# State space and wide attention of a four-layer chain: softplus first, one decay product read out of another, and reciprocal roots by Ln and Exp

## The reference

```
dt = softplus(raw_dt + dt_bias);  a = -exp(A_log) * dt
xBC = silu(depthwise_conv(xBC, 4 taps) + bias)
y[t] = sum over s <= t of exp(sum of a from s+1 to t) * (C[t] . B[s]) * dt[s] * x[s]   + D * x
out = rmsnorm(y * silu(z)) @ W_out
```

```
qh, kh = rms_norm(q @ Wq), rms_norm(kv @ Wk)        # x * rsqrt(mean(x^2) + 1e-5) * w
attn   = softmax(mask(qh @ kh^T / 8));  out = (attn @ vh) @ Wo
```

## Time and profile before

| | |
|---|---|
| median of 3 runs | 2303.56 us (2299.27 to 2307.39) |
| profiled execution, its own time | 2310.8 us |
| its span in the profile | 2309.0 us |
| granted TensorE clock, mean | 0.904 of full speed |
| busy over the span | PE 83%, DVE 69%, ACT 57%, POOL 28% |
| chain that ended last | PE 50%, DVE 31%, issue 8%, POOL 5%, ACT 5% |
| state space | about 520 to 960 us |
| wide attention | about 1383 to 1800 us |

### The profile page before, as it was taken

How to read it: one execution, slowest core, us unless ns; L and a number is a source line. 1 busy time by engine, 2 the same in 40 slices (tenths; PEclk the granted TensorE clock), 3 DMA queues, 4 the chain that set the end, 5 groups by cost and what they waited for, 6 DMA issues and landing times.

```text
span 2309.0 us, 37826 instructions
## 1 busy us (share of the span) xinstructions
PE 1907.6 (83%) x13360; PEld 1271.5 (55%) x13360; DVE 1584.6 (69%) x3689; ACT 1307.4 (57%) x2688; POOL 646.3 (28%) x616
## 2 busy tenths in 40 slices
PE   7999766979999999849864388899888997679886
PEld 5777652446777777524452254556555676434465
DVE  5777685866767767458659948888888457568543
ACT  5777433766777777517755236676665312337622
POOL 3332003104433333342004532334334001131043
PEclk9999887999999999969986689999999898779897
DMA  4000005400000000034101000000000100254112
GB/s 191 1 2 2 1 0 152 141 34 5 1 1 1 1 1 1 1 91 147 56 8 68 0 1 1 1 1 1 1 1 1 52 4 1 95 159 132 43 35 78
DMA packets 80155, 87.39 MB, mean 38 GB/s; under 512 B 6578, under 2 KB 70115, under 8 KB 79073
## 3 DMA queue, kind: packets, MB, share of 16 engines
q1 hardware_dynamic: 78625, 82.49, 11.3%
q0 software_dynamic: 1344, 2.49, 0.4%
HBM read 54.39 MB, written 30.70 MB: 37 GB/s over the span
## 4 chain that ended last, share of the span: by engine, by line
PE 50%; DVE 31%; issue 8%; POOL 5%; ACT 5%; DMA 2%; SPq 0%; DVEq 0%; POOLq 0%; ACTq 0%
PE bank L469 42%; DVE scratch L1221 5%; PE bank L653 2%; DVE scratch L3045 2%; DVE scratch L3065 2%; PE bank L368 2%; POOL w_early L3241 1%; DVE stats L245 1%; PE bank L693 1%; POOL w_early L3236 1%; DVE w_keep L1893 1%; DVE w_early L2497 1%; PE bank L1190 1%; DVE XN L3089 1%; DMA scratch<-parts 1%
## 5 line engine op out<-in xcount | busy, mean ns | idle before, releaser
L469 PE MATMUL bank<-scratch 64*128 64x256 bf16 (+7 forms) x3056 | 340.9, 307 | 83.2 <-DMA scratch<-parts 39.8
L1221 DVE TENSOR_REDUCE scratch<-bank 128x2 f32<-128x512 f32 x384 | 244.6, 686 | 83.5 <-PE bank L469 80.6
L469 PEld LDWEIGHTS bank<-scratch 64*128 64x128 bf16 (+4 forms) x3056 | 183.9, 122 | 212.1 <-DVE scratch L1221 73.6
L469 PE MATMUL bank<-w_keep,scratch 128*128 128x128 f32 (+4 forms) x1760 | 246.6, 331 | 26.8 <-DVE scratch L1936 12.1
L469 PE MATMUL bank<-XNT,w_keep 128*128 128x256 f32 (+4 forms) x800 | 238.6, 438 | 6.8 <-POOL w_keep L2131 4.6
L1307 ACT ACTIVATE w_keep<-bank 128x512 f32<-128x512 f32 x384 | 212.5, 597 | 53.6 <-PE bank L469 45.7
L469 PEld LDWEIGHTS bank<-w_keep,scratch 128*128 128x128 f32 (+3 forms) x1760 | 183.7, 185 | 92.9 <-issue 63.5
L469 PE MATMUL bank<-w_early,scratch 64*128 64x256 f32 (+3 forms) x1152 | 168.9, 355 | 42.4 <-ACT w_early L3150 26.0
L469 PEld LDWEIGHTS bank<-XNT,w_keep 128*128 128x128 f32 x800 | 150.2, 197 | 59.9 <-issue 30.4
L469 PEld LDWEIGHTS bank<-w_early,scratch 64*128 64x128 f32 (+3 forms) x1152 | 122.6, 189 | 89.2 <-issue 32.3
L469 PE MATMUL bank<-w_keep 128*32 128x256 f32 (+1 forms) x1600 | 125.2, 388 | 8.8 <-ACT w_keep L1307 5.4
(11 more groups left out here) (452 smaller groups left out, 3974.5 us busy)
## 6 DMA issues: line engine op xcount, KB each, us to landing
scratch<-parts SPq DMA_DIRECT2D x24, 1024.0 KB, 5.0
parts<-scratch SPq DMA_DIRECT2D x192, 96.0 KB, 2.5
parts<-scratch SPq DMA_DIRECT2D x96, 64.0 KB, 2.1
w_early<-pack_l3f SPq DMA_DIRECT2D x1, 5206.0 KB, 16.3
w_keep<-pack_l2f SPq DMA_DIRECT2D x1, 2124.0 KB, 12.5
w_early<-pack_mamba SPq DMA_DIRECT2D x1, 2120.0 KB, 19.2
w_keep<-pack_l2x SPq DMA_DIRECT2D x1, 2049.0 KB, 7.8
w_keep<-taps SPq DMA_DIRECT2D x4, 512.0 KB, 5.6
```

Of the source, the lines that this page charges most:

```text
L469: return pe.matmul(out, lhsT, rhs, start=start, stop=stop, skip_group_check=True)
L1221: dve.tensor_reduce(neg[:, :, h], self.k.bank[5 - g % 2][:, :].rearrange("p (t s) -> p t s", s=S), AXX, ALU.max, negate=True).then_inc(*s. ...
```

## The change

In the state space:

- The product `after` (128x4) on PE is gone. The decays up to the half's end are the last column of each head's block in bank 5, which `decay_pe` writes anyway; ACT takes their exponential there, in a new small instruction (128x4) ahead of the first `decay_act`. `late_act` reads 256 columns in place of 260. POOL's `middle_pool` waits for `decay` in place of `late`.
- Tap 0 is the unshifted one (the former tap 3), and DVE reads it straight from bank 0. The other three follow from the padded buffer. PE's next `raw_pe` waits for that DVE instruction in place of ACT's copy.
- On DVE the softplus's start and its first four series steps stand ahead of `overlap_dve`.

In the wide attention:

- Both roots are Ln and Exp(-0.5 x) on ACT; DVE's reciprocals and the keys' scaling go, and one table set (preloaded once) serves the stage.
- KS and KD are split in two pieces: KS0 in step 1, KS1 and KR in step 2, KD0 in step 3, KD1 in step 4.
- V1, V3, T01 and T11 are copied by ACT.
- POOL squares the next batch's keys ahead of its scaling in steps 0 and 1.

```
@@ state space: late_pe, tap_dve
-        mm(pe, bank[:, S:S + H_SSM], self.k.w["after"], a3[:, 0, :]).then_inc(*s.scored.up("late", u))
+        m.then_inc(*s.scored.up("late", u))
...
-            pe.wait_ge(*s.stacked.at("raw", u - 1))
+            pe.wait_ge(*s.vector.at("tap", u - 1, 0, 1))
...
-                o = dve.tensor_scalar(yv[:, j, :], xv[:, j, 0:S], scale, None, ALU.mult)
+                o = dve.tensor_scalar(yv[:, j, :], self.two(self.k.bank[0][:, :])[:, j, :], scale, None, ALU.mult)
@@ state space: dve
+            if soft:
+                soft.start_dve(dve, n)
+                soft.series_dve(dve, n, 0, 4)
             if there(prep):
                 self.overlap_dve(dve, prep)
-            if soft:
-                soft.start_dve(dve, n)
-            if there(prep):
                 self.weights_dve(dve, prep)
-            if soft:
-                soft.series_dve(dve, n, 0, 4)
@@ state space: late_act, decay_act, middle_pool
-            act.wait_ge(*s.pool.at("xu", u - 2))
-        act.activation(self.late[u % 2], self.k.bank[2][:, 0:S + H_SSM], ACT.Exp).then_inc(*s.weighed.up("late", u))
+        act.activation(self.late[u % 2][:, 0:S], self.k.bank[2][:, 0:S], ACT.Exp).then_inc(*s.weighed.up("late", u))
...
+        if t == 0:
+            if u >= 2:
+                act.wait_ge(*s.pool.at("xu", u - 2))
+            ends = columns_of(self.k.bank[5][:, :], P - 1, (P, H_SSM))
+            act.activation(self.late[u % 2][:, S:S + H_SSM], ends, ACT.Exp)
...
-        pool.wait_ge(*s.weighed.at("late", u))
+        pool.wait_ge(*s.weighed.at("decay", u, 0))
@@ wide attention: schedule
-    SCHEDULE = (("P00", "P01", "Q0"), ("P10", "P11", "Q1"), ("Q2", "Q3", "KS"), ("M", "V0", "KR", "KD"), ("B0", "V1"),
-                ("T00", "T01", "X"), ("T10", "T11", "V2", "QR", "QD"), ("B1", "V3"))
+    SCHEDULE = (("P00", "P01", "Q0"), ("P10", "P11", "Q1", "KS0"), ("Q2", "Q3", "KS1", "KR"), ("M", "V0", "KD0"), ("B0", "V1", "KD1"),
+                ("T00", "T01", "X"), ("T10", "T11", "V2", "QR"), ("B1", "V3"))
+    ON_ACT = ("V1", "V3", "T01", "T11")
@@ wide attention: score_pe, values_pe, maximum_dve
-            pe.wait_ge(*self.read(("Q3", b)))
+            pe.wait_ge(*self.read(("T10", b)))
...
+            pe.wait_ge(*self.read(("V2", b)))
...
-            dve.wait_ge(*s.rstd.at("queries", b))
+            dve.wait_ge(*s.deviation.at("queries", b))
@@ wide attention: piece_act (KR; QR the same without bias)
-            act.activation(self.kms, self.kms, ACT.Sqrt).then_inc(*s.deviation.up("keys", b))
+            act.wait_ge(*s.stats.at("keys", b, 1))
+            act.activation(self.kms, self.kms, ACT.Ln, bias=k.small[:, 0:1], scale=1.0 / HW).then_inc(*s.scalar.up("keys", b))
+            act.wait_ge(*s.scalar.at("keys", b))
+            act.activation(self.kms, self.kms, ACT.Exp, scale=-0.5).then_inc(*s.deviation.up("keys", b))
@@ wide attention: pool
-            self.scale_pool(pool, p)
             if w in (0, 1) and b + 1 < B:
                 self.squares_pool(pool, b + 1, w)
+            self.scale_pool(pool, p)
@@ wide_attention: act
-        pre_norm_act(k, e, ACT.Exp)
+        pre_norm_act(k, e)
+        e.preload_act_table_set("natural_log_exp_and_others")
```

More of the change, by code:

```diff
@@ L2861, in __init__ @@
                         self.place[name, b] = d * NWIDE + step if d >= 0 else -1
-        on_pe = [piece for piece in self.place if piece[0] not in ("KS", "KR", "KD", "QR", "QD")]
+        on_pe = [piece for piece in self.place if piece[0] not in self.UNBANKED]
         self.number = {piece: n for n, piece in enumerate(on_pe)}
@@ L3075, in piece_dve @@
         digits = [int(x) for x in name[1:] if x.isdigit()]
[L3076 to L3083, removed]
-            dve.wait_ge(*s.deviation.at("keys", b))
[L3085 to L3088, removed]
-                dve.tensor_tensor(x, x, self.kms[:, t * H:(t + 1) * H].unsqueeze(2).to_broadcast([P, H, HW]), ALU.mult).then_inc(*s.normed.up("keys", b, t))
-        elif name == "QD":
-            dve.wait_ge(*s.deviation.at("queries", b))
-            dve.reciprocal(self.qms[b % 2], self.qms[b % 2]).then_inc(*s.rstd.up("queries", b))
+        if name[0:2] == "KS":
+            t = digits[0]
+            dve.wait_ge(*s.pool.at("squares", b, t))
+            dve.tensor_reduce(self.kms[:, t * H:(t + 1) * H], self.ksquares[t].rearrange("p (h d) -> p h d", d=HW), AXX,
+                              ALU.add).then_inc(*s.stats.up("keys", b, t))
+        elif name[0:2] == "KD":
+            t = digits[0]
+            x = self.raw[t].rearrange("p (h d) -> p h d", d=HW)
+            dve.wait_ge(*s.deviation.at("keys", b))
+            dve.tensor_tensor(x, x, self.kms[:, t * H:(t + 1) * H].unsqueeze(2).to_broadcast([P, H, HW]), ALU.mult).then_inc(*s.normed.up("keys", b, t))
+        elif name in self.ON_ACT:
+            pass
         elif name[0] == "X":
@@ L3172, in piece_act @@
         if name == "KR":
-            act.wait_ge(*s.variance.at("keys", b))
-            act.activation(self.kms, self.kms, ACT.Sqrt).then_inc(*s.deviation.up("keys", b))
+            act.wait_ge(*s.stats.at("keys", b, 1))
+            act.activation(self.kms, self.kms, ACT.Ln, bias=k.small[:, 0:1], scale=1.0 / HW).then_inc(*s.scalar.up("keys", b))
+            act.wait_ge(*s.scalar.at("keys", b))
+            act.activation(self.kms, self.kms, ACT.Exp, scale=-0.5).then_inc(*s.deviation.up("keys", b))
         elif name == "QR":
             act.wait_ge(*s.formed.at("X", b))
-            act.activation(self.qms[b % 2], self.qms[b % 2], ACT.Sqrt).then_inc(*s.deviation.up("queries", b))
+            act.activation(self.qms[b % 2], self.qms[b % 2], ACT.Ln).then_inc(*s.scalar.up("queries", b))
+            act.wait_ge(*s.scalar.at("queries", b))
+            act.activation(self.qms[b % 2], self.qms[b % 2], ACT.Exp, scale=-0.5).then_inc(*s.deviation.up("queries", b))
+        elif name[0] == "V" and name in self.ON_ACT:
+            t, part = divmod(digits[0], 2)
+            act.wait_ge(*s.projected.at(*piece))
+            if b >= 2:
+                act.wait_ge(*s.summed.at("v", (b - 1) * NWIDE - 1))
+            act.activation(self.values(b)[:, t, 8 * part:8 * part + 8, :], bank[:, :].rearrange("p (h d) -> p h d", d=HW), ACT.Copy,
+                           scale=self.keep[:, b * HALVES + t:b * HALVES + t + 1]).then_inc(*s.stacked.up(*piece))
+        elif name[0] == "T" and name in self.ON_ACT:
+            t, part = digits
+            act.wait_ge(*s.projected.at(*piece))
+            if b >= 2:
+                act.wait_ge(*s.scored.at("s", (b - 1) * NWIDE - 1, 1))
+            act.activation(self.side(self.K, b)[:, 4 * part:4 * part + 4, t * P:(t + 1) * P], bank[:, :].rearrange("p (w s) -> p w s", s=P),
+                           ACT.Copy).then_inc(*s.stacked.up(*piece))
         elif name[0] == "P":
```

19 lines of the change are left out of this document (10 added, 9 removed).

## The result

The changed kernel takes 2241.3 us, median of 4 runs (2238.2 to 2246.0), against 2303.8 for the kernel before; the ratio is 0.973, with a 95% interval of 0.970 to 0.976. That is 62.5 us less, where 57 was forecast; the forecast of 2247 lies 6 us above the measurement and the range holds it. The profiled execution took 2244.2 us, its span 2242.4 (before 2309.0), at a mean granted clock of 0.911 (before 0.904).

The account below looks back on a forecast made before the run. The prediction took DVE's in-order list, partly held by POOL, to bound even state-space iterations and wide-attention batches. Gains of 22.5 and 34.5 us, 57 in all, took 2303.6 to 2247; range 2220 to 2277.

Parts of the forecast that it names:

- What left the list: State space, even iterations: the softplus's start (2.27 us) and four series steps (0.72) leave DVE's list after the overlap.
- The late overlap: State space, even iterations: the softplus, moved ahead, makes DVE's overlap start 0.15 us late.
- the tap out of the bank: State space, even iterations: reading tap 0 from the bank instead of SBUF costs 0.26 us a pair.
- the hold of the series: State space, even iterations: the last three series steps meet POOL's instructions and take 0.93 us more; bounds 0 and 1.5.
- the reopened gap: State space, even iterations: a gap ahead of the weights, which L1594 had covered, reopens and costs 0.12 us.
- ACT's limit of 2.0: State space, even iterations: with DVE out of the way, ACT's own chain limits the gain to about 2.0 us.
- The holds: Wide attention: DVE instructions standing for POOL's (L3049, KD0, KD1) give back 2.25 us a batch; bounds 0 and 4.
- The reserve that is not gained: Wide attention: DVE reached step 0's maximum late without shortening PE's list, so 1.0 us a batch is not gained.
- No holds: Both stages: moved DVE instructions do not meet POOL's or slip by; gain 81 us, to 2223; chance 0.2.
- A new wait: Both stages: half the gain goes into new waits for series steps and divided pieces; gain 27, 2276; chance 0.2.
- Nothing: Ln and Exp might each load their table set, and PE absorb DVE's gain: within 0.3%; chance 0.05.
- Slower: Wide attention: POOL's squares, ahead of its scaling, wait for ACT's copy of P01 and delay PE: 2319; chance 0.05.

Follow-up runs that it names:

- 3: The changed kernel with the softplus's start and first four series steps back behind the overlap on DVE: 2256.3 us.
- 4: The changed kernel with the product `after` back on PE, one exponential of 260 columns and the old waits: 2228.7 us.
- 9: The changed kernel with Sqrt on ACT and reciprocals on DVE for both roots, so four table loads a batch: 2246.1 us.
- 8: The changed kernel with V1, V3, T01 and T11 copied by DVE again: 2239.7 us.
- 7: The changed kernel with POOL scaling first and squaring the next batch's keys after it, as before: 2276.0 us.
- 12: The kernel before with only POOL's order changed, squaring the next batch's keys ahead of its scaling: 2295.2 us against 2301.9 beside it.
- 5: The changed kernel with the first, unshifted tap read from the padded SBUF buffer in place of the bank: 2235.3 us.
- 10: The changed kernel with KD0 and KD1 each right behind the step's maximum on DVE, ahead of the inverse: 2231.6 us.
- 11: The changed kernel with the whole softplus and decays ahead of the overlap, and KD0, KD1 right behind the maximum: 2215.0 us against 2290.1, ratio 0.969.

## Why the prediction was right

**State space: 22.5 forecast, 25.8 measured.** What left the list (2.27 and 0.72) left it, shown by 3. The late overlap was 0.10 (0.15), the tap out of the bank 0.25 (0.26), the hold of the series 1.34 - 0.58 = 0.76 (0.93). With these the sum is 1.88 less the reopened gap; the measured 1.74 leaves 0.14 for that (0.12). So the term that was too large is the hold: I let the series begin earlier against POOL's pair than it did. Its form was the forecast one, one step passing between POOL's two instructions and the next standing for the second (0.45 and 0.65). ACT's limit of 2.0 was not reached.

**The product `after`: nothing forecast, nothing measured** (4). Its cover is PE's wait for `late_act`. That ACT's new exponential costs nothing is seen in the odd iterations, unchanged at 12.98.

**Wide attention: 4.5 a batch forecast, 5.09 measured** (50.44 to 45.35). The holds came to 0.33 + 0.67 + 0.82 = 1.82 where the sum had 2.25. The reserve that is not gained was 1.97 - 1.17 = 0.80 (the maximum at 1457.22, the scores at 1456.05), and not 1.0. With both, 7.8 - 1.82 - 0.80 = 5.18. PE's floor was forecast as 43.5; PE is busy 43.52. In all, 33.4 against 31.5; seven batches of 5.09 would be 35.6. Between the masks five batches gained 25.1, 5.03 each; what lies before and behind them gained 4.4 and 3.9. DVE's list closes by its own rows as well: its idles in a batch fell from 6.53 (1.24 + 2.03 + 2.14 + 1.12) to 2.87 (0.26 + 2.03 + 0.58), 3.66 less; copies 2.6 and the small root instructions 0.7 went, holds of 1.82 came: 5.14. So the account of what bounds a batch held, and 0.4 of the 0.6 that a batch gained beyond the forecast is the holds.

**The terms of that sum are not prices of the single edits.** The wait of 1.12 for the root and the reciprocals stood in it at 1.12 + 0.35 + 0.25 = 1.72. Taking the edit back costs 1.19 (9), and another 1.24 in most batches by the clock behind PE's idle. The four copies, 2.6, cost 1.50 when they come back (8). The wait for the squares and the sum that moves, 2.14 + 1.22, cost 5.07 when POOL's order comes back (7), and the new order gives 0.90 when it alone is changed (12). The tap out of the bank stood at -0.26 against the kernel before, and taking it back in the new order costs 0.46 more (5). In-order lists with slack do not add part by part: what leaves a list is right as a sum over all of it, and wrong as the worth of one edit. What the prediction gave no term to is the low clock where PE then sets the pace: it had the slow products (1.3) as part of PE's floor alone, and that was enough for the kernel before and the changed one, not for 9.

**The prologue: 3 forecast, 1.7 measured.** It was costed by analogy with a batch and not from rows of its own. Two of its parts can be read off the experiments: it takes 20.27 with Sqrt back (9) and 20.73 with the copies back (8), where it took 19.95: 0.8 for the copies, and 0.3 for the root, which is less than kernels with the same code there differ by (19.54 to 19.99). Why these terms are smaller there than the forecast took them was not looked for.

**The rivals.** *No holds* fell by the rows of L1608, L3056 and L3092 and by 5 and 10: 2223 would need holds of zero; 11, with the largest of them moved away or made smaller, is 75 us below its neighbour, where that rival had 81. *A new wait*: no wait for a divided piece is seen; PE waits 1.15 for exponentials and twice 0.27 for scaling. *Nothing*: the table loads did vanish, 140 before and 110 after. *Slower* fell, since POOL's squares ran at 1462.45 and 1468.70, right behind the scaling before them, and never stood for ACT's copy; its price for POOL's order, 4.9 a square and so 9.8 a batch, is seen in no run. It is the old order that costs, 5.1 a batch (7).

## What to carry to other kernels

Work that fills a gap which an in-order list has anyway is worth its whole duration, and its price is where it meets the other engine of the shared port: lay the two timelines over each other and count the overlap in tenths of a microsecond, for every moved instruction and for those behind it. When several edits of one list share its slack, forecast the list's end as a whole, and take no single edit's price from it; an edit that gives little alone (0.9 us here) can be the one on which all the others hang. Where PE idles, look at the granted clock of the step behind, and at who waits for that step: the lower clock cost nothing in the kernel before, where DVE's list was the bound, and 1.2 to 2.9 us a time where DVE came to wait for PE.

## What the runs showed of the hardware

**The clock after short idles.** The kernel before, step 5 of a batch, behind idles of PE of 2.94 and 2.47 us with 5.9 us of work between:

```profile
1528.91:1535.09 6.18, 6.18 (x36) 4.54 (x36) 5.97 (x15) 3.51 (x8) 2.64 (x2) 0.72 0.00 0
```

The granted clock is 0.72 over this step, so part of it ran at the lower of the two levels, 1.2 GHz; the steps on either side of it were at 1.00. In the next batch it was step 4 instead, at 0.65, behind the idle of 2.94. It is 0.77 in 7 behind an idle of 3.16, 0.77 and 0.63 in 9 behind 2.65 (and 1.00 once behind the same 2.65), 0.72 in 12 behind 2.47 (and 1.00 once), and 1.00 over every batch of the changed kernel. But long idles are not all there is to it. In 3, whose wide attention is that of the changed kernel, step 5 of the first batch was at 0.73 behind an idle of 1.74, which the changed kernel has at 1.00. And in the last batch of 7, 10 and 11 two steps were at 0.71 to 0.73 behind idles of 0.90 and 1.29. The same products behind the same idle, in 10 and in the changed kernel:

```profile
1683.36 1.82 PE L2934 MATMUL bank<-w_keep,w_early 128*128 128x128 f32 x8 [1.29 <-POOL w_early L3265]
...
1689.61 1.09 PE L2934 MATMUL bank<-w_keep,w_early 128*128 128x128 f32 x8 [1.29 <-POOL w_early L3261]
```

What decides between the two is not shown.

PE's busy time of a batch fell by 44.75 - 43.52 = 1.23 us, by the products' durations in the slow step; the prediction had priced it from two slow rows (1.3). Time is another matter. In the kernel before, a batch with a mean clock of 0.93 took 50.23 us, like others at 0.97, and in 12 one at 1.00 took 49.46 between two at 0.97 of 49.32: the low clock cost nothing. In 9 it cost 1.24 and 2.68, and in the last batch of 10 it cost 2.9, with DVE waiting 1.85 and 1.82 for PE's scores.

**Which DVE instructions are held.** With POOL's 1.77 running, a pair of 256 columns took 2.10 from SBUF (5) and 0.87 from a bank; ones of 16 columns (L1598, 0.98) and of 2 (L3056, 0.82) with two inputs in SBUF stood until POOL's was done, like the wide divisions (1.89 and 2.04). Not every DVE instruction that reads SBUF is held, as the prediction had it: the sum L3086 (TENSOR_REDUCE) took its usual 1.21, from 1467.28 to 1468.49, though POOL's L3261 ran from 1466.85 to 1468.74. A waiting one gets in between two POOL instructions that follow one another directly, one at a time (0.45 and then 0.65 for two steps of L1608, 0.98 and 0.65 for L1598 and L1600). The lock is stated by the page SBUF — State Buffer of the Trainium skill, cited in the prediction; that one slips through was seen here.

**ACT on few columns.** 128x4 out of a bank took 0.17 us (L2015), 128x256 0.36 to 0.38 (L2004).
